# A gate by two token tiles, stack transfers in two parts, and rank counts in five matmuls

## The reference, cut to what matters

```
x = x + gnn(layernorm(x), adj)            # 16 x 512 x 256
    q, k, v = x @ Wq.T, x @ Wk.T, x @ Wv.T
    attn = softmax(where(adj != 0, q @ k.T / sqrt(32), -inf))
    c = attn @ v
    gate = sigmoid(concat([c, x]) @ Wg.T + bg)
    return gate * x + (1 - gate) * c
x = x + ffn(layernorm(x))
    w, idx = top_k(softmax(flat @ router_w), 2);  w = w / sum(w)
    out = sum over the two experts of w * (silu(x @ Wg[e]) * (x @ Wu[e])) @ Wd[e]
    out = out + (silu(x @ Sg) * (x @ Su)) @ Sd
```

## Time and profile before

| | |
|---|---|
| median of 3 runs | 1842.68 us (1841.36 to 1845.65) |
| the profiled execution's own time | 1845.24 us |
| its span, first to last instruction | 1843.5 us |
| PE busy / PEld busy | 1739.2 us (94%) / 1459.3 us (79%) |
| DVE / ACT / POOL busy | 1272.6 (69%) / 1101.4 (60%) / 654.2 us (35%) |
| mean granted PE clock | 0.985 |

### The profile page before, as it was taken

One profiled execution on the slowest core, in us unless ns is written; L12 is line 12 of the kernel. 1 busy time (PEld: TensorE's weight loads), 2 busy tenths in 40 slices (PEclk: granted clock), 3 DMA queues, 4 the chain that ended last, 5 costly groups with the idle time before them and its releaser, 6 DMA issues. The chain is left out here.

```text
span 1843.5 us, 36156 instructions
## 1 busy us (share of the span) xinstructions
PE 1739.2 (94%) x12613; PEld 1459.3 (79%) x12613; DVE 1272.6 (69%) x3153; ACT 1101.4 (60%) x2509; POOL 654.2 (35%) x479
## 2 busy tenths in 40 slices
PE   5999999899999999999799999999999999999996
PEld 4677777677777777777587888788888988898986
DVE  5667777777776777777554564577778777877773
ACT  4888888888888888888533333233444443434442
POOL 0135444345544444553230100014433343344334
PEclk8999999999999999999899999999999999999998
DMA  5444565555455555555232354346546556555553
GB/s 148 132 141 130 159 171 169 151 155 149 146 166 161 164 164 156 148 147 166 81 104 92 115 172 149 127 161 166 167 139 171 137 163 167 161 165 162 135 151 38
DMA packets 140947, 269.21 MB, mean 146 GB/s; under 512 B 15072, under 2 KB 92256, under 8 KB 135776
## 3 DMA queue, kind: packets, MB, share of 16 engines
q1 hardware_dynamic: 113760, 230.45, 40.6%
q0 software_dynamic: 26592, 35.67, 9.5%
q10 hardware_dynamic: 416, 0.79, 0.2%
HBM read 141.99 MB, written 74.52 MB: 117 GB/s over the span
## 5 line engine op out<-in xcount | busy, mean ns | idle before, releaser
L836 DVE CUSTOM_DVE_ANT_0 pf<-bank,bias_q 128x512 f32<-128x512 f32 x512 | 348.0, 687 | 207.2 <-PE bank L480 194.3
L1188 POOL DMA_INDIRECT out_x<-yb,ix x142 | 245.1, 1726 | 570.8 <-ACT yb L1412 465.9
L609 ACT ACTIVATE pf<-pf,nmax 128x512 f32<-128x512 f32 x512 | 373.4, 729 | 50.5 <-DVE nmax L836 45.4
L1424 ACT ACTIVATE ah<-am 128x512 fp32r<-128x512 f32 (+1 forms) x220 | 133.1, 605 | 441.2 <-DVE am L1492 439.7
L1323 PE MATMUL bank<-xh,wh 128*128 128x512 f32 (+1 forms) x880 | 337.0, 383 | 0.9 <-ACT pt L597 0.9
L490 PE MATMUL bank<-ident,pf 128*128 128x128 f32 x2048 | 312.6, 275 | 26.0 <-ACT pt L597 25.3
L1324 PE MATMUL bank<-xl,wh 128*128 128x512 f32 (+1 forms) x880 | 336.3, 382 | 0.0
L1325 PE MATMUL bank<-xh,wl 128*128 128x512 f32 (+1 forms) x880 | 336.2, 382 | 0.0
L490 PEld LDWEIGHTS bank<-ident,pf 128*128 128x128 f32 x2048 | 252.5, 141 | 82.6 <-issue 35.8
L597 ACT ACTIVATE pt<-bank 128x512 f32<-128x512 f32 x512 | 307.2, 600 | 12.9 <-PE bank L490 12.8
L480 PE MATMUL bank<-stack 96*128 96x512 f32 x512 | 237.1, 463 | 31.4 <-DMA stack<-qk 16.6
(11 more groups left out here) (209 smaller groups left out, 3147.6 us busy)
## 6 DMA issues: line engine op xcount, KB each, us to landing
raw<-in_w_all SPq DMA_DIRECT2D x39, 1536.0 KB, 6.8
stack<-qk SPq DMA_DIRECT2D x378, 128.0 KB, 2.4
xb<-xg_dram SPq DMA_DIRECT2D x32, 520.0 KB
adj_i<-in_adj SPq DMA_DIRECT2D x32, 512.0 KB, 5.1
xn<-in_x SPq DMA_DIRECT2D x16, 512.0 KB, 6.4
xn_dram<-xn SPq DMA_DIRECT2D x16, 512.0 KB
xp<-in_x SPq DMA_DIRECT2D x16, 512.0 KB, 6.7
xnp<-xn_dram SPq DMA_DIRECT2D x16, 512.0 KB, 7.9
```

What stands on the lines that cost most here:

```text
L609: act.activation(pf[i][:, :], pf[i][:, :], ACT.Exp, bias=nmax[:, i:i + 1], scale=-1.0, accum_out=den[:, g, tq, j:j + 1]).then_inc(p_exp, 1)
L836: dve.tensor_tensor_reduce(pf[r][:, :], S[p % 2][:, :], bias_q[1 - par][:, tq, :], -SCALE, -3.0 * MASKED, ALU.add, ALU.min, nmax[:, r:r + ...
L1188: pool.indirect_dma_start(out=out, out_offset=bass.IndirectOffsetOnAxis(ap=ix[n % RING][:, i:i + 1], axis=0), in_=yb[s][:, i, :], in_offse ...
```

## The change

Three edits. (1) The gate and x1 are computed in two halves of two token tiles each: gate at slots 17 and 19, x1 at 18 and 20, statistics of x1 at 19 and 21 in place of 21 and 22; `s_mix` counts 4 a batch in place of 2. Beside it the four `bn_stats` of the next x move from slot 8 to slot 12, ahead of their variance. (2) In `end(b)` SP waits for K0's high part and Q0's low part, sends (QH, KH) and (QL, KH) of heads 0 to 3, then waits for K0's low part and sends (QH, KL) of the four heads. The first batch keeps its way. (3) R0's fourteen matmuls become five over all four tiles: one of 32 columns with the triangle, three of 24, 16 and 8 columns with all ones and a tile's counts repeated, one of 32 columns for the earlier batches.

```diff
-DVE_AT = {..., "stat": 8, "var": 12, ..., "gate": 19,
-          "x1": 20, "stat2": 21, "var2": 23}
+DVE_AT = {..., "stat": 12, "var": 12, ..., "gate": (17, 19),
+          "x1": (18, 20), "stat2": (19, 21), "var2": 23}
...
-        def send_head(eng, r):
+        def send_head(eng, r, part=range(3)):
             m, j = r // HPT, r % HPT
-            for rows, (a, c) in enumerate([(QH, KH), (QL, KH), (QH, KL)]):
+            for rows in part:
+                a, c = [(QH, KH), (QL, KH), (QH, KL)][rows]
...
-                    refs(B, unit(b, "K0") + 1, range(0, GRP, 2) if first(b) else range(GRP))
+                    if first(b):
+                        refs(B, unit(b, "K0") + 1, range(0, GRP, 2))
+                    else:
+                        sp.wait_ge(g_free, unit(b, "Q0") + 1)
+                        sp.wait_ge(g_hi, hi_index(b, "K0") + 1)
+                        sp.nop().then_inc(s_held_sp, 1)
+                        for r in range(GRP):
+                            send_head(sp, r, range(2))
+                        sp.wait_ge(g_free, unit(b, "K0") + 1)
+                        for r in range(GRP):
+                            send_head(sp, r, range(2, 3))
...
-                    for i in range(NT):
-                        pe.matmul(o[:, E * i:E * i + E], below[:, :], mb[:, i, :], start=True, stop=False)
-                        for j in range(i):
-                            pe.matmul(o[:, E * i:E * i + E], ones_b[:, :], mb[:, j, :], start=False, stop=False)
-                        last = pe.matmul(o[:, E * i:E * i + E], ones_b[:, :], msum[:, :], start=False, stop=True)
+                    oe = o[:, 0:NT * E].rearrange("p (i e) -> p i e", e=E)
+                    pe.matmul(oe, below[:, :], mb[:, :, :], start=True, stop=False)
+                    for j in range(NT - 1):
+                        pe.matmul(oe[:, j + 1:NT, :], ones_b[:, :],
+                                  mb[:, j:j + 1, :].to_broadcast([P, NT - 1 - j, E]), start=False, stop=False)
+                    last = pe.matmul(oe, ones_b[:, :], msum[:, :].rearrange("p (o e) -> p o e", o=1)
+                                     .to_broadcast([P, NT, E]), start=False, stop=True)
...
+                for half in range(2):
+                    hs = slice(half * NT * D // 2, (half + 1) * NT * D // 2)
+                    if post and p == DVE_AT["gate"][half]:
+                        dve.wait_ge(g_free, unit(b, "Z3" if half else "Z1") + 1)
+                        dve.wait_ge(s_d, A * 2 + 2)
+                        dve.scalar_tensor_tensor(out=df[:, hs], in0=zf[:, hs], scalar=1.0, in1=df[:, hs],
+                                                 op0=ALU.add, op1=ALU.mult).then_inc(s_mix, 1)
+                    if post and p == DVE_AT["x1"][half]:
+                        dve.wait_ge(s_mix, A * 4 + 2 * half + 1)
+                        x1f = x1[:, :, :].rearrange("p i d -> p (i d)")
+                        dve.scalar_tensor_tensor(out=x1f[:, hs], in0=df[:, hs], scalar=0.5, in1=x1f[:, hs],
+                                                 op0=ALU.mult, op1=ALU.add).then_inc(s_mix, 1)
+                    if post and p == DVE_AT["stat2"][half]:
+                        dve.wait_ge(s_mix, A * 4 + 2 * half + 2)
+                        statistics(x1, stats2, s_stat2, A * (2 * NT + 1), (2 * half, 2 * half + 1))
```

More of the change, by code:

```diff
@@ L28 @@
 ACT_AT = {"exp": 5}
-DVE_AT = {"choose": 3, "mark": 4, "weigh": 6, "place": 14, "stat": 8, "var": 12, "bias0": 4, "bias1": 16, "gate": 19,
-          "x1": 20, "stat2": 21, "var2": 23}
+DVE_AT = {"choose": 3, "mark": 4, "weigh": 6, "place": 14, "stat": 12, "var": 12, "bias0": 4, "bias1": 16, "gate": (17, 19),
+          "x1": (18, 20), "stat2": (19, 21), "var2": 23}
 POOL_AT = {"diff": 8, "x1": 10, "rstd": 12, "xn": 13, "rstd2": 24, "xn2": 25}
@@ L374, in end @@
                     dyn = not isinstance(A, int)
-                    sp.wait_ge(s_mix, A * 2 + 2)
+                    sp.wait_ge(s_mix, A * 4 + 4)
                     sp.dma_start(x1_t[bass.ds(A, 1)].rearrange("o p i d -> p (o i) d")
@@ L710, in low @@
                 elif name[0] == "X":
-                    dve.wait_ge(s_mix, A * 2 + 1)
+                    dve.wait_ge(s_mix, A * 4 + 3)
                     dve.nop().then_inc(s_held_dve, 1)
@@ L870, in at @@
                     scores_mask(b, par, 0 if p == DVE_AT["bias0"] else 1)
-                if post and p == DVE_AT["gate"]:
-                    dve.wait_ge(g_free, unit(b, "Z3") + 1)
-                    dve.wait_ge(s_d, A * 2 + 2)
-                    dve.scalar_tensor_tensor(out=df[:, :], in0=zf[:, :], scalar=1.0, in1=df[:, :],
-                                             op0=ALU.add, op1=ALU.mult).then_inc(s_mix, 1)
-                if post and p == DVE_AT["x1"]:
-                    dve.wait_ge(s_mix, A * 2 + 1)
-                    x1f = x1[:, :, :].rearrange("p i d -> p (i d)")
-                    dve.scalar_tensor_tensor(out=x1f, in0=df[:, :], scalar=0.5, in1=x1f,
-                                             op0=ALU.mult, op1=ALU.add).then_inc(s_mix, 1)
-                if post and p in (DVE_AT["stat2"], DVE_AT["stat2"] + 1):
-                    second = p - DVE_AT["stat2"]
-                    dve.wait_ge(s_mix, A * 2 + 2)
-                    statistics(x1, stats2, s_stat2, A * (2 * NT + 1), (2 * second, 2 * second + 1))
+                for half in range(2):
[13 more added lines that the diff above has]
+                        statistics(x1, stats2, s_stat2, A * (2 * NT + 1), (2 * half, 2 * half + 1))
                 if post and p == DVE_AT["var2"]:
@@ L949, in at @@
                     if p == POOL_AT["diff"]:
-                        pool.wait_ge(s_mix, A * 2)
+                        pool.wait_ge(s_mix, A * 4)
                         pool.tensor_tensor(diff[:, :, :], xnp[:, :, :], c_tok[:, :, :],
```

## The result

The changed kernel takes 1822.14 us (median of 4 runs, 1820.48 to 1825.82), beside 1843.89 us (1841.36 to 1845.65) of the kernel before on the same chip: a ratio of 0.9889, 95% interval 0.9869 to 0.991. It is faster by 21.7 us, inside the predicted range of 1802 to 1828; the forecast itself, 1811.7, promised 31 us. The question is where the other 9 us are. The profiled execution took 1823.27 us with a span of 1820.5 us, 22.0 us less than the profiled one of before.

The account below looks back on a forecast made before the run. PE was taken as the attention bound except at four places a batch. Gains of 16.7 + 3.5 + 6 + 3 + 2 = 31 us off the 1842.68 us median gave 1811.7 us, range 1802 to 1828.

Parts of the forecast that it names:

- The four places: Where PE is not the bound in an attention batch: slots 8 to 12, 19 to 28, next batch's 0 to 3, and 4.
- Part 1: bn_stats moved from slot 8 to 12: 1.19 us in each of 14 batches, 16.7 us, bounds 11 and 17.
- Part 2: Five rank matmuls for fourteen at slot 12: 0.25 us in each of 14 batches, 3.5 us, bounds 0 and 4.
- Part 3: Gate and x1 in halves: ACT's 0.39 us idle before exponential 24 goes, 6 us in all, bounds 0 and 10.
- Part 4: Stack in two parts: the wait at slots 1 to 3 moves to slot 0, gaining 0.2 us a batch, 3 us.
- the adjacency's term: Store and loads in `begin` leave SP up to 1.7 us earlier, shortening late adjacency waits: 2 us in all.
- (a): Rival: ACT bounds earlier, the gate gives nothing and slot 12's second wait stays: 1823 us; chance 0.22 together with (b).
- (b): Rival: slot 12 pays back, tile 13's minimum and C1's low part stop PE: 1817 to 1823; 0.22 with (a).
- (c): Rival: the stack's earlier start reaches slot 0 and no wait is left: 1800 us; chance 0.10.
- (d): Rival: ninth stack transfer late at slot 0, 2.7 us, costing 29 us: end at 1840; chance 0.08, half over 1846.
- (e): Rival: the edits don't do what they say: within 5 us of the sum; counted in the forecast's 0.60.
- The signs named in advance: Tile 10 to 13 about 5.0 us, ranks 0.13, no ACT idle before exponential 24, slot 0 waits 0.4, batches 51 to 52.

Follow-up runs that it names:

- e1: The kernel before with one edit, the four bn_stats of the next x at slot 12 in place of 8: 1841.38 us, ratio 0.999.
- h1: The changed kernel with the store of xn held until tile 21's scores are done: 1812.95 us, ratio 0.9857.
- h3: The changed kernel with bn_stats at slot 10 and the variance at slot 11, both from 12: 1814.06 us, ratio 0.9865.
- e4: The kernel before with only gate, x1 and the statistics of x1 in halves, bn_stats still at slot 8: 1832.61 us, ratio 0.9939.
- e3: The kernel before with only the stack transfers in two parts: 1835.68 us, ratio 0.9959.
- i3: The kernel before with one more wait, POOL's rstd held until tile 14's scores are done: 1868.2 us, ratio 1.0133.

## Why the prediction was right or wrong

**What bounds the kernel:** right. The four places were the ones where time went, and slots 13 to 19 and 28 to 30 didn't move.

**Part 1, bn_stats.** The local sum was right: slots 10 to 13 gave 1.28 us alone (e1) and 1.49 with the ranks, where 1.19 and 1.44 were put, and nothing was late at slot 12. The step that failed is the sentence "POOL's scatters are queued behind xn and move with it; they are needed a batch later". It asked only whether what moved would be in time, xn for P0 and the scatters for the next batch, and both were. It put no price on what the moved work would stand beside. That price was 0.9 us a batch at slot 20 alone in e1, where all but 3 us of the forecast 16.7 were gone, and 0.73 us at slots 20 to 23 of the changed kernel (0.94 up to slot 27, against h1 and h3). It also said nothing of the store of xn, the other thing that waits for xn, on SP's queue: the chain was followed on POOL alone.

**Part 2, ranks.** 0.21 to 0.23 us a batch in place of 0.25. From the first rank matmul to L524 it takes 0.21 us, not 0.13: the prediction's 5 x 0.026 left out that 0.10 us pass between the last one's start and L524, before as after. The argument from L511 was weak, since its 32 matmuls start in groups of four some 0.2 us apart and not one each 0.058 us, but its result holds: the starts of the five are under 0.03 us apart at 24 and 32 columns as they were at 8. The Trainium skill (TensorE: Matmul & The Clock Gate, "Wait — 56ns, not 53.3ns?") puts its lower bound of about 25 ns there; the trace agrees, now for these widths too.

**Part 3, gate.** The mechanism was right, the size mis-sized: 0.39 us was taken, 0.62 us is what e4, h1 and h3 gain in slots 24 to 27. The step that failed is "The minimum of tile 22 doesn't move": it comes 0.23 us earlier, and ACT's other idle time, before exponential 22, shrinks by 0.22 us. In the changed kernel 0.41 is left of the 0.62, where tiles 20 to 23 come late; that it equals the prediction there is chance.

**Part 4, stack.** The wait moved to slot 0 as said; it was 0.87 us there in batch 13, not 0.4, with landings of 2.3 to 3.0 us, and 0.7 us in the mean over batches 1 to 14, slow issues included, as its sum had (0.7 to 0.8). The net by slots was 0.14 to 0.19 us a batch for 0.20, too small against what the place varies by to confirm it. With the adjacency's term it was forecast at 5 us; the time of e3 says 7.6, with 3.9 as the lower bound. DVE's waits for the adjacency did go, the 3.33 us at slot 4 among them; how much of that reached PE is not shown.

**The rivals.** (a) falls: ACT's exponentials were not the bound, the gate gave more than said. (b) falls at slot 12, no minimum and no L493 waits there; its 1817 to 1823 is near the result by another mechanism. (c), the stack clearly better, and (d), slower by the ninth transfer, fall: slot 0 waited 0.7 us in the mean where (d) had 2.7. (Its "eight at once" in flight does not fit: at one issue each 0.64 us and 2.3 us to landing it is about four.) (e) falls, each part did what it says. That the result lies between the forecast and (a) comes from a cost that none of them names. That it lies in the range is in part luck: the range was opened for (a) and (b), and neither came.

**The signs named in advance.** 5.07 us for 5.0 from tile 10 to tile 13; none of the waits on DVE at tile 11; no idle time before exponential 24; batches of 52.0 to 53.8 us, 52.7 in the mean, for 51 to 52. From the first rank matmul to L524 it took 0.21 us for 0.13. Of the signs named as wrong one came twice: at slot 0 PE waited over 1.5 us for the stack in batches 1 and 5 (2.3 and 1.6 us). The others didn't (ACT's emptying stopped PE at slot 12 in 13 batches of before and in none of after; P0 never waited for POOL in batches 2 to 14), and the list had no sign for a result that PE had made and the others didn't get.

**The version that is best.** h3 (1814.06 us, ratio 0.9865) and h1 (1812.95, 0.9857), against 0.9889 of the changed kernel: the intervals overlap, so by these runs alone 4 to 6 us are not settled. In the slots they are, by one trace each: both take 51.95 us for a batch in place of 52.69. h3 needs no wait, only two numbers. What is late next in both is the stack: PE waits for it 12.8 us in 18 places of h3 between 100 and 860 us.

## What to carry to other kernels

When a step moves, price the place where its followers land, on every queue, not only whether they are in time: here 0.9 of the 1.28 us gained at slots 10 to 13 in e1 was returned at slot 20, beside a store and eight scatters that nobody waits for there. Slot lengths from one trace against the other's, all 32 of them, find such a place in minutes, since the slots that should not have changed are the control. And where the profile put waits down to nothing it knows, on three engines at once, the result was there late; the waiting engines were not slow.

## What the hardware showed that I had not expected

- PE's results can reach other engines late though the matmul that made them started on time: 3.2 us from tile 20's start to DVE's in batch 4 of after (2.6 in the mean) and 3.4 us in i3, where 1.6 us (h1, DVE busy until then) and 0.6 us are usual. In the same stretch PE's own run of 32 matmuls (L524) is stretched from 1.86 us to 2.22 in the mean of after and 2.76 in e1, with no wait in the program inside it. The Trainium skill (Perfetto Trace Analysis, "Tensor Engine Instruction (MATMUL, LD_WEIGHTS)") says that a matmul's end in the profile is an estimate and that its semaphore is raised once PSUM has taken all bytes; so the row of a matmul can look whole while its signal is late, which is what tile 20's row in the traces here shows (0.48 us long in after as in h1).
- A single wait put on POOL, 2.1 us long and needed by nobody at that point, cost 24 us (i3).
- In about two of three batches one of SP's twelve stack issues takes 1.2 to 2.2 us in place of 0.6, in after as in before (9 and 10 of 14 batches).
